# Delta stage of a four-layer kernel: a new order by hand for the products of q and the gate, the output products, the sums z, the norms and the alpha spread

## The chip, the cores and the metric

The kernel runs on one core of a Trainium2 chip. The metric is device time in microseconds (us) of one launch, the median of several. Engines: PE is TensorE (matmul), DVE VectorE, ACT ScalarE, POOL GpSimd, SP the engine whose queue issues most transfers.

## The reference

Four layers, each followed by a residual sum and a layer norm. The first is a gated delta rule over x (8 batches, 1024 steps, width 512):

```
q, kr, v = x @ Wq + bq, x @ Wk + bk, x @ Wv + bv          # 128 wide
k = kr / max(norm(kr), 1e-12)
alpha, beta, gate = sigmoid(x @ Wa + ba), sigmoid(x @ Wb + bb), sigmoid(x @ Wg + bg)
S_new = a * (S - b * outer(S k, k)) + b * outer(v, k)     # one step
o = (q @ S_new) * gate
x1 = layernorm(x + o @ Wo + bo)
```

Then three blocks of 4-bit weights with a low-rank term; an attention whose values are zero by its shapes (HD equals ROPE, so it adds nothing to x); and a low-rank MLP.

## The kernel before, in words

The first part of the program, the **delta stage** (`delta_rule_and_weights`), computes x1 and turns the packed weights into float tiles; a second part runs the two MLPs, and its code isn't changed.

The delta stage takes the 1024 steps in 8 chunks of 128 (`CHUNKS`) and the 8 batches in 2 groups of 4 (`GB`, `GROUPS`). One chunk of one group is a **unit**, numbered n = 2c + g, 0 to 15. Every engine runs the same list of pieces, `ORDER`, once per unit, taking the pieces that it has code for, in that order and without overtaking; semaphores tie the engines. In `ORDER` a word `U.0'` with one mark belongs to the unit before (n - 1), with two marks to the one before that (n - 2); so each pass works on three units. `ORDER` is used for units 0 to 13 (2 to 13 in a hardware loop of two units a turn), `ORDER_PREVIOUS` for unit 14 and `ORDER_LAST` for unit 15, both with pieces of the weights' preparation added; `TAIL` follows.

The pieces that matter here:
- xT: 4 transposes of x on PE for a batch s (L883), waiting for the load of `x_in[g]`; ACT and DVE take the high and low halves. kv: 12 products (L895 to L899) into bank `p_pj[s % 2]`; sq and copy: ACT empties it.
- root, diag, kh: 1 / norm of k and khat. DVE makes the floor (L721), POOL the power (L511) and beta's diagonal (L527), DVE khat (L742). **decay** is the alpha spread: PE spreads alpha (L939) into `p_wide` (h = 0) or `p_pj[1]` (h = 1), and DVE scans it into DT (L729) and A (L734).
- kT, kk, MnT, M, W0: the triangular system of the chunk. M (L976) transposes it, W0 ends in M_both on DVE; part.2 to part.6 are five masks of it on POOL (L533), then kA (L541) and qA (L548) follow on POOL.
- The **levels** 1 to 6 invert it by doubling. In each, PE does Y (L1003) and T (L990), ACT copies both out, PE does X (L1011), DVE adds it in (L786), and the next level's Y waits for that. `inverse` is the last half level.
- KS', U', PT', S', O': the chunk's result og for the unit before, and its new state S on DVE. ogT': og split in high and low halves by ACT and POOL (L552).
- q and g: 12 products each of 512 columns (L905), into `p_pj[0]` and `p_pj[1]`; qout and gout: ACT empties them.
- attn.s': 3 products with Wo (L1090 to L1092) for a batch s, into `p_pj[s % 2]`. z.s': DVE adds the residual (L830). stats.s: DVE's mean and variance, POOL's rstd. norm.s: DVE's `(z - mean) * rstd` in place (L843).
- residual pieces: POOL adds bo to `x_res` (L567), one with each of KS', U', PT' and S'.

The SP queue, in order, in a turn of the loop:

```
load(c + 1, 0); load(c + 1, 1)              # x_in
store(c, 0); load_residual(c + 1, 0)        # a store waits for each norm
store(c, 1); load_residual(c + 1, 1)
```

so the loads of `x_in` for units 2c + 4 and 2c + 5 stand behind the last norm of unit 2c + 1, which is done in unit 2c + 3. After the loop, ahead of the loads for unit 14 stands `load_rows(0)`, and the end of unit 15's queue is: `store(6, 1)` (the norms of unit 13), its residual, lora_b (`lb`), a wait for unit 15's g products, `load_rows(3)`, three loads of lora_a (`la`). ACT's pieces `la_hi` wait for these.

Of the kernel before, what the change touches and what calls it, by code (L numbers as in the profile page):

```python
# [117 lines left out]
def delta_rule_and_weights(nc, x, w, consts, masks, x1, q, kept):  # L118
# [22 lines left out]
    with nc.cleanup_on_exit(), ExitStack() as ctx:  # L141
# [146 lines left out]
        def order(text):  # L288
# [24 lines left out]
        def with_more(more):  # L313
# [11 lines left out]
        G_PIECES = [("g", i, 0) for i in range(3 * KT)] + [("gout", 0, 0)]  # L325
        ORDER_LAST = [piece for piece in with_more({
# [16 lines left out]
        def tail(text):
# [11 lines left out]
            stats.2' lbT.0 stats.3' lbT.1 U tile.0.0 norm.2' norm.3' lbT.2 PT low.0.0 tile.0.1 S low.0.1 tile.0.2 O low.0.2 tile.0.3 lbT.3 low.0.3  # L355
# [26 lines left out]
        def ring_free(eng, *piece):  # L382
# [114 lines left out]
        def _(pool):  # L497
# [89 lines left out]
        def _(act):  # L587
# [112 lines left out]
        def _(dve):  # L700
# [112 lines left out]
            def O(c, g, _):  # L813
# [4 lines left out]
                for s in range(GB if state_used(c) else 0):  # L818
                    dve.wait_ge(s_["S_ps"], 2 * n + s // 2 + 1)
# [44 lines left out]
            run(dve, {"xT": xT, "root": root, "decay": decay, "kh": kh, "A": A_, "MnT": MnT_, "W0": X0, "Y": Y, "X": X, "inverse": inverse, "KS": KS, "U": U, "PT": PT_, "O": O,  # L864
# [3 lines left out]
        def _(pe):  # L868
# [1166 lines left out]
```

## Time and profile before

| | us |
|---|---|
| median of 3 runs (range) | 2453.42 (2453.25 to 2454.66) |
| the profiled execution | 2452.19 |
| its span | 2450.40 |
| delta stage: to the end of unit 15 | 695.8 |
| tail of the weights' preparation | 695.8 to 738.3 |
| second part | 739.8 to 2450.4 |
| PE busy in the span | 2321.4 (95%) |
| DVE, ACT, POOL busy | 1590.2, 1146.5, 766.8 |

The span runs from the first to the last instruction of the profiled execution; its own time has 1.79 us around that. Busy time of PE is modelled to the end of each matmul, so neighbours overlap and a short gap shows only where PE really waited. "Idle before <- X" names what released an engine. A unit is counted from one unit's first transpose of x to the next one's.

### The profile page before, as it was taken

The page shows a single profiled execution, that of the slowest core. Times are in us where ns is not written, and L with a number is a line of the kernel's source. Part 1 is how long each engine was busy: PE and PEld are TensorE (multiplying, and loading weights), DVE is VectorE, ACT ScalarE, POOL GpSimd, SP SyncE. Part 2 cuts the span into 40 slices and gives each one's busy share as a digit, 9 for nine tenths or more (in the row PEclk, how much of TensorE's full clock was granted, in tenths as well). Part 3 has the DMA queues.
Part 4 walks back from the last instruction along what each step waited for, and adds up shares of the span by engine and source line. Part 5 has one row for each costly group of instructions (what it writes and reads, how often), then busy time and mean ns, then how long its engine had stood idle before and what let it go on. Part 6 is the DMA issues. An engine that isn't in the chain of part 4 may idle for free.

```text
span 2450.4 us, 37424 instructions
## 1 busy us (share of the span) xinstructions
PE 2321.4 (95%) x12333; PEld 1931.0 (79%) x12333; DVE 1590.2 (65%) x3002; ACT 1146.5 (47%) x2289; POOL 766.8 (31%) x1200
## 2 busy tenths in 40 slices
PE   6898888888879999999999999999999999999997
PEld 5787777877767888888888888888888878888886
DVE  3656565656676666666666766667676666666666
ACT  3333333333244433435344353443534477777775
POOL 2344444444441121111211112111120135555555
PEclk8999999999989999999999999999999999999999
DMA  5122122122340020100201002010021233333222
GB/s 133 52 70 82 55 93 78 43 94 94 102 153 1 18 87 1 69 34 17 86 0 68 34 17 86 0 68 34 17 94 39 86 100 112 115 114 107 103 86 69
DMA packets 101706, 166.14 MB, mean 68 GB/s; under 512 B 19664, under 2 KB 22480, under 8 KB 101520
## 3 DMA queue, kind: packets, MB, share of 16 engines
q1 hardware_dynamic: 97328, 163.69, 19.8%
q10 hardware_dynamic: 4320, 1.71, 0.3%
q8 instruction: 32, 0.52, 0.1%
q14 instruction: 26, 0.21, 0.0%
HBM read 115.05 MB, written 50.33 MB: 67 GB/s over the span
## 4 chain that ended last, share of the span: by engine, by line
PE 67%; DVE 1%; POOL 1%; issue 0%; DVEq 0%; ACT 0%; POOLq 0%
PE quant_bank L1512 7%; PE quant_bank L1511 7%; PE quant_bank L1510 7%; PE quant_bank L1900 6%; PE quant_bank L1902 6%; PE quant_bank L1901 6%; PE quant_bank L1538 5%; PE quant_bank L1537 5%; PE quant_bank L1539 5%; PE quant_bank L1527 3%; PE quant_bank L1556 2%; PE quant_bank L1558 2%; PE quant_bank L1557 2%; PE quant_bank L1499 1%; PE quant_bank L1917 1%; PE quant_bank L1568 1%
## 5 line engine op out<-in xcount | busy, mean ns | idle before, releaser
L1351 POOL TENSOR_SCALAR quant_var<-quant_mv 128x1 f32<-128x1 f32 x256 | 57.0, 223 | 1007.1 <-DVE quant_mv L1426 1007.1
L1379 ACT ACTIVATE quant_g_hi<-quant_bank,kept_beta,kept_gamma 128x512 fp32r<-128x512 f32 x192 | 150.7, 785 | 395.5 <-PE quant_bank L1527 395.4
L1510 PE MATMUL quant_bank<-kept_W_hi,quant_h_hi 128*128 128x512 f32 x768 | 305.4, 398 | 0.0
L1511 PE MATMUL quant_bank<-kept_W_lo,quant_h_hi 128*128 128x512 f32 x768 | 303.5, 395 | 0.0
L1512 PE MATMUL quant_bank<-kept_W_hi,quant_h_lo 128*128 128x512 f32 x768 | 303.4, 395 | 0.0
L1424 DVE BATCH_NORM_STATS2 quant_stats<-quant_bank 128x6 f32<-128x512 f32 x192 | 134.0, 698 | 196.3 <-PE quant_bank L1512 196.3
L1865 DVE TENSOR_TENSOR mlp_g_lo<-quant_bank,mlp_g_hi 128x512 fp32r<-128x512 f32 x256 | 176.4, 689 | 105.7 <-ACT quant_bank L1802 105.3
L1801 ACT ACTIVATE mlp_g_hi<-quant_bank,mlp_b 128x512 fp32r<-128x512 f32 x256 | 177.3, 693 | 70.6 <-PE quant_bank L1902 63.5
L1537 PE MATMUL quant_bank<-quant_g_hi,kept_W_hi 128*128 128x512 f32 x512 | 205.2, 401 | 0.0
L1538 PE MATMUL quant_bank<-quant_g_hi,kept_W_lo 128*128 128x512 f32 x512 | 202.5, 396 | 0.0
L1539 PE MATMUL quant_bank<-quant_g_lo,kept_W_hi 128*128 128x512 f32 x512 | 202.4, 395 | 0.0
L1446 DVE TENSOR_TENSOR quant_g_lo<-quant_bank,quant_g_hi 128x512 fp32r<-128x512 f32 x192 | 130.3, 689 | 100.1 <-ACT quant_bank L1380 97.9
L1394 ACT ACTIVATE quant_bank<-kept_b_all 128x512 f32<-128x512 f32 x192 | 113.2, 603 | 133.1 <-DVE quant_y L1439 74.3
L1512 PEld LDWEIGHTS quant_bank<-kept_W_hi,quant_h_lo 128*128 128x128 f32 x768 | 144.0, 187 | 35.1
L1511 PEld LDWEIGHTS quant_bank<-kept_W_lo,quant_h_hi 128*128 128x128 f32 x768 | 144.1, 188 | 34.1
L1510 PEld LDWEIGHTS quant_bank<-kept_W_hi,quant_h_hi 128*128 128x128 f32 x768 | 144.0, 188 | 34.1
L1802 ACT ACTIVATE quant_bank<-quant_bank,mlp_b 128x512 f32<-128x512 f32 x256 | 168.2, 657 | 0.0
L1439 DVE TENSOR_SCALAR quant_y<-quant_bank,quant_mv,quant_rstd 128x512 f32<-128x512 f32 x192 | 155.6, 810 | 17.3 <-POOL quant_rstd L1353 17.3
L1353 POOL TENSOR_TENSOR quant_rstd<-quant_var,quant_minus_half 128x1 f32<-128x1 f32 x256 | 141.3, 552 | 21.3
L1380 ACT ACTIVATE quant_bank<-quant_bank,kept_beta,kept_gamma 128x512 f32<-128x512 f32 x192 | 145.4, 757 | 0.0
L1389 ACT ACTIVATE quant_h_hi<-kept_x_in 128x512 fp32r<-128x512 f32 x128 | 81.9, 640 | 123.6 <-DVE kept_x_in L1458 99.7
L1760 POOL TENSOR_SCALAR mlp_z<-mlp_z,mlp_mv,mlp_rstd 128x512 f32<-128x512 f32 x60 | 124.0, 2079 | 0.0
(277 smaller groups left out, 5889.6 us busy)
## 6 DMA issues: line engine op xcount, KB each, us to landing
delta_x_in<-L_attn_x_d SPq DMA_DIRECT2D x16, 1024.0 KB, 8.0
delta_x_res<-L_attn_x_d SPq DMA_DIRECT2D x16, 1024.0 KB, 5.4
x_d<-delta_z SPq DMA_DIRECT2D x64, 256.0 KB, 2.1
kept_x_in<-x_d SPq DMA_DIRECT2D x16, 1024.0 KB, 5.3
quant_y<-x_d SPq DMA_DIRECT2D x16, 1024.0 KB, 5.2
x_d<-quant_y SPq DMA_DIRECT2D x16, 1024.0 KB, 4.2
mlp_x_in<-x_d SPq DMA_DIRECT2D x16, 1024.0 KB, 10.4
mlp_x_res<-x_d SPq DMA_DIRECT2D x16, 1024.0 KB, 6.5
```

What stands on the lines that cost most here:

```text
L1379: nc.scalar.activation(g_hi[m][:, k, :], tr[k][:, :], ACT.Gelu, bias=beta[:, b, k:k + 1], scale=gamma[:, b, k:k + 1])
L1439: nc.vector.tensor_scalar(y[m][:, e, :], lin_of["up", m, b, e][:, :], mv[m][:, e, 0:1], rstd[m][:, e:e + 1], ALU.subtract, ALU.mult).then_ ...
L1510: mm(out, x_hi, W_hi[2 * b][:, k, :], start=False, stop=False, skip_group_check=True)
L1511: mm(out, x_hi, W_lo[2 * b][:, k, :], start=False, stop=False, skip_group_check=True)
L1512: last = mm(out, x_lo, W_hi[2 * b][:, k, :], start=False, stop=k == KT - 1, skip_group_check=True)
L1537: mm(out, W_hi[2 * b + 1][:, k, cols], g_hi[m][:, k, :], start=k == 0, stop=False)
L1538: mm(out, W_lo[2 * b + 1][:, k, cols], g_hi[m][:, k, :], start=False, stop=False)
L1539: last = mm(out, W_hi[2 * b + 1][:, k, cols], g_lo[m][:, k, :], start=False, stop=k == KT - 1)
L1801: nc.scalar.activation(g_hi[:, at, :], p_h[at][:, :], ACT.Gelu_apprx_tanh, bias=b1[:, f:f + 1])
L1802: nc.scalar.activation(p_h[at][:, :], p_h[at][:, :], ACT.Gelu_apprx_tanh, bias=b1[:, f:f + 1]).then_inc(s_["gelu_done"], 1)
L1865: nc.vector.tensor_tensor(g_lo[:, at, :], p_h[at][:, :], as_f32(g_hi[:, at, :]), ALU.subtract).then_inc(s_["g_lo_done"], 1)
L1900: mm(out, lhs[0], rhs[0], start=first, stop=False)
```

## The change

- `ORDER` is written anew. The 12 products of q (now single pieces) stand in threes between kk, decay.1, kT.1, M.0 and kk.1; the 12 of g follow, all ahead of level 1. The output products attn', now three pieces each, stand two to a level in levels 1 to 5 and two in level 6; z' stands in levels 2, 4, 5 and behind `inverse`, stats.0' and stats.1' in levels 3 and 5.
- decay.0 stands behind S' and kv.2, where it stood ahead of S'. norm.0'' and norm.1'' stand behind xT.3, norm.2'' and norm.3'' in level 1, behind X.1.1. The four updates of S become pieces new_S.0 and new_S.1, with root.1 between them.
- The waits for the banks `p_pj` follow the new order: attn.0 and attn.1 wait for q and the gate of the next unit to be out, the seeds of kv for z.2 and z.3 of two units before.
- `ORDER_LAST` no longer moves g into level 1. la_hi.0 stands behind X.2.0 (it stood behind X.4.1), la_hi.1 behind X.3.0.
- The SP queue's code and the engine of the norm (DVE, L843) are not changed.

```diff
         ORDER = order("""
-            xT.0 xT.1 KS.0' kv.0 stats.0'' stats.1'' stats.2'' sq.0 copy.0 U.0' xT.2 kv.1 norm.0'' stats.3'' norm.1'' sq.1 copy.1 ab.0 PT.0' xT.3 root.0 diag.0 decay.0 kh.0
-            norm.2'' norm.3'' S.0' O.0' kv.2 sq.2 copy.2 kT.0 ogT.0' A.0 kv.3 sq.3 copy.3 root.1 ab.1 diag.1 kk.0 attn.0' MnT.0 z.0' decay.1 attn.2' kh.1 kT.1 M.0 z.2' W0.0 kk.1 q.0 q.1 A.1 MnT.1 q.2 q.3 M.1 qout.0 W0.1 attn.1'
-            part.2 part.3 part.4 part.5 part.6 kA.0 z.1' attn.3' qA.0
-            Y.1.0 T.1.0 Y.1.1 T.1.1 z.3' X.1.0 X.1.1
-            Y.2.0 T.2.0 Y.2.1 T.2.1 g.0 X.2.0 X.2.1 g.1
-            Y.3.0 T.3.0 Y.3.1 T.3.1 g.2 X.3.0 X.3.1 g.3
-            Y.4.0 T.4.0 Y.4.1 T.4.1 g.4 X.4.0 X.4.1 g.5
-            Y.5.0 T.5.0 Y.5.1 T.5.1 g.6 X.5.0 X.5.1 g.7
-            Y.6.0 T.6.0 Y.6.1 T.6.1 g.8 g.9 inverse.0 inverse.1 g.10 g.11 gout.0""")
+            xT.0 xT.1 KS.0' kv.0 sq.0 copy.0 stats.2'' U.0' xT.2 kv.1 sq.1 copy.1 ab.0 root.0 diag.0 stats.3'' PT.0' xT.3 norm.0'' norm.1''
+            S.0' kv.2 sq.2 copy.2 decay.0 kh.0 A.0 O.0' kT.0 kv.3 sq.3 copy.3 new_S.0' root.1 ab.1 diag.1 new_S.1' ogT.0'
+            q.0 q.1 q.2 kk.0 MnT.0 decay.1 q.3 q.4 q.5 kh.1 kT.1 A.1 M.0 q.6 q.7 q.8 W0.0 kk.1 q.9 q.10 q.11 qout.0 MnT.1 g.0 g.1 g.2 M.1 g.3 g.4 g.5 W0.1
+            part.2 part.3 part.4 part.5 part.6 kA.0 g.6 g.7 g.8 g.9 g.10 g.11 qA.0 
+            Y.1.0 T.1.0 Y.1.1 T.1.1 gout.0 attn.0.0' X.1.0 X.1.1 norm.2'' norm.3'' attn.0.1'
+            Y.2.0 T.2.0 Y.2.1 T.2.1 attn.0.2' X.2.0 X.2.1 z.0' attn.1.0'
+            Y.3.0 T.3.0 Y.3.1 T.3.1 attn.1.1' X.3.0 X.3.1 stats.0' attn.1.2'
+            Y.4.0 T.4.0 Y.4.1 T.4.1 attn.2.0' X.4.0 X.4.1 z.1' attn.2.1'
+            Y.5.0 T.5.0 Y.5.1 T.5.1 attn.2.2' X.5.0 X.5.1 z.2' stats.1' attn.3.0'
+            Y.6.0 T.6.0 Y.6.1 T.6.1 attn.3.1' attn.3.2' inverse.0 inverse.1 z.3'""")
...
-        G_PIECES = [("g", i, 0) for i in range(3 * KT)] + [("gout", 0, 0)]
-        ORDER_LAST = [piece for piece in with_more({
+        ORDER_LAST = with_more({
             ("norm", 1, 2): dequants((1, 0)),
             ("norm", 3, 2): dequants((1, 1)),
             ("kh", 0, 0): dequants((1, 2), (1, 3)),
             ("X", (1, 1), 0): dequants((2, 0)),
-            ("X", (2, 0), 0): [("stats", 0, 1)],
+            ("X", (2, 0), 0): [("la_hi", 0, 0)],
             ("X", (2, 1), 0): dequants((2, 1)),
-            ("X", (3, 0), 0): [("norm", 0, 1)],
-            ("X", (3, 1), 0): [("stats", 1, 1), ("lb_hi", 0, 0), ("lb_hi", 1, 0)],
+            ("X", (3, 0), 0): [("la_hi", 1, 0)],
+            ("stats", 0, 1): [("la_lo", 0, 0), ("lb_hi", 0, 0), ("lb_hi", 1, 0)],
             ("X", (4, 0), 0): dequants((2, 2)) + [("lb_hi", 2, 0), ("lb_lo", 0, 0)],
-            ("X", (4, 1), 0): [("norm", 1, 1), ("la_hi", 0, 0), ("la_lo", 0, 0)],
-            ("X", (5, 0), 0): dequants((2, 3)) + [("la_hi", 1, 0), ("la_lo", 1, 0)],
-            ("X", (5, 1), 0): dequants((3, 0)) + [("la_hi", 2, 0), ("la_lo", 2, 0)],
-            ("inverse", 0, 0): [("la_hi", 3, 0), ("la_lo", 3, 0), ("KS", 0, 0)]}) if piece not in G_PIECES]
-        at = ORDER_LAST.index(("X", (1, 1), 0)) + 1
-        ORDER_LAST[at:at] = G_PIECES
+            ("z", 1, 1): [("norm", 0, 1), ("la_lo", 1, 0), ("la_hi", 2, 0)],
+            ("X", (5, 0), 0): dequants((2, 3)) + [("la_hi", 3, 0)],
+            ("stats", 1, 1): dequants((3, 0)) + [("la_lo", 2, 0)],
+            ("inverse", 0, 0): [("la_lo", 3, 0), ("norm", 1, 1), ("KS", 0, 0)]})
...
-            stats.2' lbT.0 stats.3' lbT.1 U tile.0.0 norm.2' norm.3' lbT.2 PT low.0.0 tile.0.1 S low.0.1 tile.0.2 O low.0.2 tile.0.3 lbT.3 low.0.3
+            stats.2' lbT.0 stats.3' lbT.1 U tile.0.0 norm.2' norm.3' lbT.2 PT low.0.0 tile.0.1 S new_S.0 new_S.1 low.0.1 tile.0.2 O low.0.2 tile.0.3 lbT.3 low.0.3
...
                 elif bank is p_pj[0]:
-                    eng.wait_ge(s_["q_done"], GROUPS * CHUNKS)
+                    eng.wait_ge(z_done[2], GROUPS * CHUNKS - 1)
                 elif bank is p_pj[1]:
-                    eng.wait_ge(s_["g_done"], GROUPS * CHUNKS)
+                    eng.wait_ge(z_done[3], GROUPS * CHUNKS - 1)
...
             def la_lo(c, g, l):
                 pool.wait_ge(w_["la_hi_done"], l + 1)
-                pool.wait_ge(w_["lb_lo_done"], 1)
-                pool.wait_ge(s_["rstd_done"], GB * (GROUPS * CHUNKS - 2) + min(l + 1, 2) if l < EARLY else GB * GROUPS * CHUNKS)
+                if l >= 1:
+                    pool.wait_ge(w_["lb_lo_done"], 1)
+                pool.wait_ge(s_["rstd_done"], GB * (GROUPS * CHUNKS - 2) + 1 + l // 2 if l < EARLY else GB * GROUPS * CHUNKS)
...
                 if s < 2:
-                    wait(act, s_[("q_done", "g_done")[s]], n)
+                    wait(act, z_done[2 + s], n - 1)
...
                 dve.wait_ge(s_["O_ps"], n + 1)
                 nc.vector.tensor_tensor(og[:, :, :], small, gate[g][:, :, :], ALU.mult).then_inc(s_["og_done"], 1)
 
-                for s in range(GB if state_used(c) else 0):
-                    dve.wait_ge(s_["S_ps"], 2 * n + s // 2 + 1)
+            def new_S(c, g, h):
+
+                if not state_used(c):
+                    return
+                n = GROUPS * c + g
+                dve.wait_ge(s_["S_ps"], 2 * n + h + 1)
+                for s in (2 * h, 2 * h + 1):
                     nc.vector.scalar_tensor_tensor(S[g][:, s, :, :], S[g][:, s, :, :], A[g][:, s, P - 1:P], pair[s // 2][:, s % 2, :, :],
                                                    ALU.mult, ALU.add).then_inc(s_["S_done"], 1)
...
-            def q_(c, g, k):
-
-                n = GROUPS * c + g
-                if k == 0:
+            def q_(c, g, i):
+
+                n = GROUPS * c + g
+                if i == 0:
                     pe.wait_ge(s_["xT_lo_done"], GB * n + GB)
                     pe.wait_ge(s_["kv_done"], GB * n + 3)
-                    wait(pe, z_done[2], n)
-                for part in range(3):
-                    last = columns_product(p_q, Q_OF, k, part)
-                if k == KT - 1:
+                last = columns_product(p_q, Q_OF, i // 3, i % 3)
+                if i == 3 * KT - 1:
                     last.then_inc(s_["q_ps"], 1)
 
             def g_(c, g, i):
@@ -922,7 +924,6 @@
                 if i == 0:
                     pe.wait_ge(s_["xT_lo_done"], GB * n + GB)
                     pe.wait_ge(s_["A_done"], GB * n + GB)
-                    wait(pe, z_done[3], n)
                 last = columns_product(p_g, G_OF, i // 3, i % 3)
                 if i == 3 * KT - 1:
...
-            def attn(c, g, s):
-
-                n = GROUPS * c + g
-                pe.wait_ge(s_["ogT_lo_done"], n + 1)
-                if s >= 2:
-                    pe.wait_ge(z_done[s - 2], n + 1)
-                elif not isinstance(n, int) or n < GROUPS * CHUNKS - 1:
-                    if s == 0:
-                        pe.wait_ge(s_["kv_done"], GB * (n + 1) + 3)
+            def attn(c, g, at):
+
+                s, part = at if isinstance(at, tuple) else (at, None)
+                n = GROUPS * c + g
+                if not part:
+                    pe.wait_ge(s_["ogT_lo_done"], n + 1)
+                    if s >= 2:
+                        pe.wait_ge(z_done[s - 2], n + 1)
+                    elif not isinstance(n, int) or n < GROUPS * CHUNKS - 1:
+                        pe.wait_ge(s_[("q_done", "g_done")[s]], n + 2)
                     else:
-                        pe.wait_ge(s_["A_done"], GB * (n + 1) + GB)
-                else:
-                    ring_read(pe, p_pj[s % 2], EARLY_PIECES)
+                        ring_read(pe, p_pj[s % 2], EARLY_PIECES)
                 out = p_pj[s % 2][:, :]
-                mm(out, ogT_hi[:, s, :], wo_hi[:, :], start=True, stop=False)
-                mm(out, ogT_hi[:, s, :], wo_lo[:, :], start=False, stop=False)
-                mm(out, ogT_lo[:, s, :], wo_hi[:, :], start=False, stop=True).then_inc(attn_ps[s], 1)
+                for i, (weights, moving) in enumerate(((ogT_hi, wo_hi), (ogT_hi, wo_lo), (ogT_lo, wo_hi))):
+                    if part is None or i == part:
+                        last = mm(out, weights[:, s, :], moving[:, :], start=i == 0, stop=i == 2)
+                        if i == 2:
+                            last.then_inc(attn_ps[s], 1)
```

## Rows read from the trace of the kernel before

**Rows 1.** Windows: us, busy PE, PEld, DVE, ACT, POOL (instructions), granted clock, DMA share, GB/s.

```profile
54.70:94.80 40.10, 36.78 (x261) 32.60 (x260) 19.96 (x50) 14.81 (x50) 12.89 (x16) 1.00 0.08 28
94.80:600.10 505.30, 446.62 (x3122) 392.39 (x3121) 306.83 (x744) 177.74 (x600) 223.94 (x312) 1.00 0.22 77
600.10:643.30 43.20, 36.79 (x261) 32.56 (x260) 27.41 (x67) 14.82 (x50) 19.07 (x26) 1.00 0.23 74
643.30:695.80 52.50, 41.93 (x250) 35.47 (x249) 34.56 (x74) 18.91 (x58) 28.69 (x33) 0.90 0.41 113
739.80:2450.40 1710.60, 1695.25 (x8064) 1384.98 (x8064) 1148.91 (x1966) 882.57 (x1446) 450.55 (x767) 1.00 0.17 60
```

**Rows 2.** Waits, 94.8 to 600 us: who waited for whom, total us, times, longest.

```profile
PE delta_p_wide L939 <- DVE delta_PT L811: 21.1, 12, 1.8
PE delta_p_pj L1090 <- DVE delta_z L830: 20.1, 24, 0.9
PE delta_p_pj L1090 <- POOL delta_ogT_lo L552: 9.7, 12, 0.9
```

**Rows 3.** Timeline of PE in unit 9: start us, us, what, [idle before <- releaser].

```profile
393.64 1.13 PE L1037 MATMUL delta_p_pair<-delta_XZ,delta_bR 128*128 128x128 f32 x8 [0.16 <-DVE delta_bR L800]
...
407.08 0.65 PE L899 MATMUL delta_p_pj<-delta_w_hi,delta_xT_lo 128*128 128x258 f32 x4
...
411.71 0.44 PE L952 MATMUL delta_p_tr<-kept_ident,delta_khat 128*128 128x128 f32 x2
...
415.94 0.27 PE L976 MATMUL delta_p_tr<-kept_ident,delta_MnT 128*128 128x128 f32 x1
...
418.74 0.40 PE L1003 MATMUL delta_p_wide<-delta_XZ,delta_M_both 128*128 128x128 f32 x2
...
422.99 0.47 PE L1003 MATMUL delta_p_wide<-delta_XZ,delta_L 128*128 128x128 f32 x2
...
425.05 0.47 PE L1003 MATMUL delta_p_wide<-delta_XZ,delta_L 128*128 128x128 f32 x2
...
431.96 1.03 PE L883 MATMUL delta_p_tr<-kept_ident,delta_x_in 128*128 128x128 f32 x8
```

**Rows 4.** Timeline of DVE in unit 9.

```profile
397.38 1.16 DVE L843 TENSOR_SCALAR delta_z<-delta_z,delta_mv,delta_rstd 128x512 f32<-128x512 f32 x1
...
404.63 0.99 DVE L843 TENSOR_SCALAR delta_z<-delta_z,delta_mv,delta_rstd 128x512 f32<-128x512 f32 x2
...
411.26 0.40 DVE L742 TENSOR_TENSOR delta_khat<-delta_kvab,delta_rn 128x256 f32<-128x256 f32 x1
...
424.62 0.69 DVE L786 TENSOR_TENSOR delta_XZ<-delta_p_pair,delta_XZ 128x128 f32<-128x128 f32 x2 [1.37 <-PE delta_p_pair L1011]
```

**Rows 5.** Timelines of POOL (unit 9), then DVE, POOL and ACT (unit 15).

```profile
420.37 1.27 POOL L541 TENSOR_TENSOR delta_qkA<-delta_qkT,delta_A 128x512 f32<-128x512 f32 x1
...
675.57 1.30 DVE L856 SCALAR_TENSOR_TENSOR delta_rows<-delta_rows,delta_scale 128x512 f32<-128x512 int32 x1
...
676.27 1.75 POOL L548 TENSOR_TENSOR delta_qkA<-delta_qkT,delta_A 128x512 f32<-128x512 f32 x1
...
687.92 0.63 ACT L685 ACTIVATE delta_la_early<-delta_la_st_early 96x512 fp32r<-96x512 f32 x1 [2.82 <-DMA delta_la_st_early<-L_ffn_lora_a_d]
```

**Rows 6.** Timeline of SP's queue, in unit 9 and in unit 15.

```profile
407.30 1.03 SPq L437 DMA_DIRECT2D delta_x_in<-L_attn_x_d  x2
...
659.57 0.45 SPq L440 DMA_DIRECT2D delta_x_res<-L_attn_x_d  x1
...
678.42 0.37 SPq L450 DMA_DIRECT2D delta_rows<-L_ffn_qweights_d  x1
```

**Rows 7.** Tile views, landings: x_in issued 407.30; x_in issued 575.49; lb issued 660.46.

```profile
DMA to landing us min/median/max: 6.9/6.9/6.9
...
DMA to landing us min/median/max: 9.8/9.8/9.8
...
DMA to landing us min/median/max: 6.6/6.6/6.6
```

More of the change, by code:

```diff
@@ L862, in low @@
                 nc.vector.tensor_tensor(kept.W_lo[l][:, j, :], ring_bank("tile", i)[:, :], as_f32(kept.W_hi[l][:, j, :]), ALU.subtract).then_inc(w_["W_lo_done"], 1)
-            run(dve, {"xT": xT, "root": root, "decay": decay, "kh": kh, "A": A_, "MnT": MnT_, "W0": X0, "Y": Y, "X": X, "inverse": inverse, "KS": KS, "U": U, "PT": PT_, "O": O,
+            run(dve, {"xT": xT, "root": root, "decay": decay, "kh": kh, "A": A_, "MnT": MnT_, "W0": X0, "Y": Y, "X": X, "inverse": inverse, "KS": KS, "U": U, "PT": PT_, "O": O, "new_S": new_S,
                       "z": z_, "stats": stats_, "norm": norm, "unit": unit_, "dequant": dequant, "low": low})
```

## The prediction, made before the changed kernel was run

> **What bounds the kernel now.** I read the windows first. PE is busy in 1695 of 1711 us of the second part, which the change doesn't touch; the delta stage is where PE idles [rows 1]. Units 2 to 13 take 505.3 us, 42.1 each, of which PE is busy 446.6, 37.2 each: 4.9 us a unit are gaps. The waits over the same 12 units say what ends them [rows 2]: decay.0 waits for PT_done of the unit before (21.1 us), attn.2 and attn.3 for z.0 and z.1, whose banks they write over (20.1), attn.0 for POOL's half of og (9.7). These make 50.9 us, 4.2 a unit. The other 0.7 is small: 0.2 where U' waits for KS' [rows 3], the rest at kk.1 and at level 2. Last comes the timeline of one unit in the middle of the loop (unit 9): where on PE's order each wait lies, and in the levels how little room there is. A level takes 2.06 us from Y to Y [rows 3]; PE has work throughout, and X, DVE's addition and the next Y follow each other closely, so a late DVE lengthens a level at once. DVE has 1.37 us free between the additions of two levels [rows 4].
>
> **The 4.2 us.** All three waits go. decay.0 comes 3.3 us of PE's work (S' and kv.2) later, and its 1.8 us wait is shorter than that. attn' starts in level 1, over 6 us after og was split, and two levels lie between a z and the product that waits for it. The wait at kk.1 goes too, as six products now lie between kT.1, M.0 and it. No matmul is added or taken away, so PE's 37.2 stays.
>
> **The filler in the levels.** Before, a level held two products of g; now two of the output products, with the same 512 columns, so the level stays 2.06. On DVE, z takes 0.7 us and a statistics piece about 0.9, under the 1.37 free. Only level 5 has both, and behind it comes the longer gap ahead of `inverse`. ACT's gout (0.7) is in level 1, where ACT waits over 1 us. I cost these at nothing.
>
> **kT.1 becomes a wait.** Behind kv.3 runs a chain: ACT's square, DVE's floor, POOL's power and diagonal, DVE's decay.1 and kh.1, PE's kT.1. Before, it took from the last part of kv.3 at 407.08 (ended by about 407.6) to 411.71, 4.1 us, of which 0.35 was a z that DVE did ahead of decay.1 [rows 3]. PE spent them on kk.0, attn.0, decay.1 and attn.2. Now there are only q.0 to q.5, kk.0 and decay.1: 6 x 0.23 and the short ones, 2.3 us. In the chain the floor no longer meets a POOL operation (saves 0.3 to 0.4), but ogT on POOL now runs beside kh.1, which was 0.40 alone [rows 4] and will be some 0.4 more. Chain 3.7, less 2.3: a new wait of 1.4 us (1.0 to 1.8).
>
> **The norms in level 1 collide with POOL.** This is the step that I weigh most. A norm alone takes 0.5 us (two took 0.99), but the one at 397.38, with a residual addition running on POOL, took 1.16 [rows 4]. In unit 15 a DVE operation at 675.57, behind kA, took 1.30, and qA, issued meanwhile, took 1.75 where kA takes 1.27 [rows 5]. So these two engines shut each other out for whole operations. Where do they meet now? M.1 was at 415.94 and kA at 420.37, 4.4 later, with POOL running without a break from the masks on [rows 3, 5]. In the new order nine g products lie between M.1 and Y.1.0, so Y.1.0 (call it Y) is 2.4 behind M.1 and kA runs from Y + 2.0 to Y + 3.3, then qA. X.1.1 reaches DVE at about Y + 2.1, norm.2'' issues at Y + 2.3: it waits for kA and ends at Y + 3.6. qA has been issued, takes 1.2 more, and norm.3'' ends at Y + 5.0. Only then can DVE add X.2.0, due at Y + 3.7. Level 2 is 1.25 us longer. The low end is 0.3: norm.3'' slips in ahead of qA, or norm.2'' ahead of kA (0.25 us decides that); two such DVE operations in a row against waiting POOL work are not in the trace. I take 1.25, as qA in unit 15 started as soon as its one blocker ended.
>
> The Trainium skill ("SBUF — State Buffer", section "Who interferes with whom") says that the pair of ports these engines share is an exclusive lock, that whoever issues first has it for the whole instruction, and that the other fully blocks. By that rule qA, issued ahead of norm.3'', goes first, and the unit would be 1.25 longer; without a lock it would be 0. This trace agrees on one blocked operation (1.16 against 0.5).
>
> **A unit of the loop**: 37.2 + 0.2 (U') + 1.4 (kT.1) + 1.25 (level 2) = 40.05, against 42.1: 2.05 less, times 12 = **-24.6**.
>
> **Loads of x_in.** The norms are later in the unit, and the loads stand behind them on SP. Before, the last norm ended at 405.6 and x_in was issued at 407.30 and landed 6.9 later [rows 4, 6, 7]: 8.6 after the norm. Now that is Y + 5.0 + 8.6 = Y + 13.6. The next unit starts at Y + 13.2 (418.74 to 431.96 [rows 3]) less 0.55 for the two g that stood behind `inverse`, less 0.1, plus 1.25: Y + 13.8. It just fits; for five such starts I allow **+0.5** in all. The residual's load lands earlier still, and POOL needs it no sooner.
>
> **Units 0 and 1** have no norms of earlier units. Unit 1: 40.1 before [rows 1], PE's 36.8 + 1.6 now, -1.7. Unit 0 waits at the same places, but has no output products to fill the levels when its g leave them; I guess it by unit 1 at -1.5. Together **-3.2** (-1 to -5).
>
> **Unit 14** took 43.2, of which 1.1 was dequantisation on DVE, and that stays; one more in level 1 costs 0.5. Its x_in has 1 MB of packed weights in front and landed 9.8 instead of 6.9 after its issue [rows 7]: with no slack left, 2.9. So 40.05 + 1.1 + 0.5 + 2.9 = 44.5, **+1.3**.
>
> **Unit 15** took 52.5. ACT's la_hi.0 was in level 4 and waited 2.82 us for lora_a, to 687.92 [rows 5]. Now it is in level 2, and ACT's copies for level 3 are behind it. On SP, lora_a stands behind the norms of unit 13, now in level 1, a residual, lora_b and 1 MB of weights. With Y at 27.5 from the unit's start (26.2 by the other units, 1.3 for dequantisation) and one dequantisation more ahead of the norms, the last norm ends at Y + 5.8 and the residual is issued at Y + 6.25 = 33.8. From there to lora_b's landing is 0.9 + 6.6 = 7.5 us (659.57, 660.46 and the landing [rows 6, 7]), and from the weights' issue at 678.42 to lora_a's landing was 9.5. One behind the other these make 17.0; if their queueing hides more, 13.5. I take 15.5: lora_a lands at 49.3. From there to the end of unit 15 was 7.9 us; two levels more make 4.2, ACT's and POOL's preparation pieces, now bunched, 0.5. Its end was DVE's, 0.6 behind PE's new boundary: 49.3 + 12.6 - 0.6 = 61.3. **+8.8** (+5 to +13). The tail has the same pieces and transfers: 0.
>
> **The sum.** -24.6 + 0.5 - 3.2 + 1.3 + 8.8 = -17.2. On the profiled execution's 2452.2 that is 2435.0. The median of the runs is 1.2 above it, so I say **2436.0**.
>
> **Rivals.**
> - *The norms hardly collide* (0.3 instead of 1.25): 0.95 x 12 = 11.4 less, 2425. For: a quarter of a us decides; with the kT.1 wait at its low end 2420. Against: POOL is busy without a break there. Chance 0.27.
> - *The ends are dearer*: lora_a at 17.0 and PE at half clock behind the long stall (the clock was 0.90 of full over unit 15, with a stall of 2.8 there [rows 1, 5]), the kT.1 wait 1.8: +1.5 +2 +4.8, 2444. Chance 0.17.
> - *Slower*: x_in lands late at every second unit. Its price is the time that it is late, six times. It decides from (17.2 + 4.9) / 6 = 3.7 us: then the kernel is slower. For: the slack is 0.2. Against: landings of 6.9 repeat, and nothing else moves data then. Chance 0.04.
> - *Nothing*: the two together come near zero, from x_in late by 2.1 us up, or DVE work in levels 2 to 5 adding 0.3 to each. Chance 0.06.
>
> The forecast itself has 0.46. Its own range is 2430 to 2441. The range that leaves out 2 in 10 reaches into the first two rivals: **2421 to 2448**. About 0.2% (4.9 us) is what a measurement can tell from no change; faster 0.90, same 0.06, slower 0.04.
>
> **What would show it.** In the changed profile: no wait of decay.0, attn.0, attn.2 and attn.3 in the loop; a wait of about 1.4 us ahead of kT.1 that DVE's khat ends; norms at L847 or so of 1.2 us or more in level 1, and a gap of 1.2 us on PE at Y.3.0; units of 40.0; a first transpose in unit 14 that waits for x_in; ACT in unit 15 waiting over 12 us for lora_a, and PE behind it. I am wrong if the norms meet POOL otherwise than counted, if a unit's start waits for x_in throughout, or if lora_a comes much sooner or later than 49 us into unit 15.

## The result, and the profile after

The changed kernel takes **2415.23 us** (median of 4 runs, 2414.15 to 2416.22). The kernel before, run beside it, takes 2454.04 (4 runs, 2453.25 to 2457.15): a ratio of 0.9839 (95% interval 0.9822 to 0.9856), 38.8 us less. I had said 2436.0, range 2421 to 2448: the direction was right, and the time lies below the range. The profiled execution took 2414.36 with a span of 2412.6, so 37.8 of the span's 2450.4 are gone.

Windows of the kernel after: unit 1, units 2 to 13 with the wait ahead of unit 14, unit 14, unit 15, the second part; and below them unit 9 by itself. They answer to [rows 1].

```profile
50.90:87.50 36.60, 35.12 (x262) 32.52 (x262) 20.68 (x54) 14.92 (x50) 13.27 (x18) 1.00 0.10 30
87.50:552.50 465.00, 427.63 (x3123) 390.35 (x3122) 328.55 (x747) 179.12 (x600) 230.09 (x316) 1.00 0.23 82
552.50:595.10 42.60, 37.33 (x260) 33.69 (x261) 30.00 (x65) 14.92 (x50) 16.60 (x23) 0.96 0.25 90
595.10:657.40 62.30, 38.89 (x254) 34.46 (x253) 35.88 (x72) 19.73 (x59) 26.95 (x32) 0.84 0.31 92
701.70:2412.60 1710.90, 1694.93 (x8064) 1384.45 (x8064) 1149.56 (x1966) 882.52 (x1446) 448.49 (x767) 1.00 0.18 60
...
357.11:395.48 38.37, 35.58 (x262) 32.52 (x262) 27.29 (x63) 14.93 (x50) 18.97 (x27) 1.00 0.26 94
```

What ended PE's waits in units 2 to 13 (us in total, times, longest), for [rows 2]:

```profile
PE delta_p_tr L953 <- DVE delta_khat L741: 17.1, 12, 1.4
PE delta_p_wide L1004 <- DVE delta_XZ L785: 14.6, 12, 1.2
PE delta_p_tr L887 <- DMA delta_x_in<-L_attn_x_d: 1.3, 2, 0.8
```

| | forecast | measured | from |
|---|---|---|---|
| a unit of the loop | 40.05 | 38.4 | starts of the units |
| of it: gap at U' | 0.2 | 0.14 | unit 9 |
| gap ahead of kT.1 | 1.4 | 1.44 | unit 9 |
| gap ahead of Y.3.0 | 1.25 | 1.22 | unit 9 |
| **PE's work without gaps** | **37.2** | **35.6** | unit 9; 427.63 / 12 |
| x_in late in the loop, 12 units | +0.5 | +1.3 | waits |
| units 0 and 1 | -3.2 | -7.5 | 79.2 against 86.7 |
| x_in of unit 14 late | +2.9 | +2.7 | timeline |
| unit 14 itself | -1.6 | -0.7 | 42.6 against 43.3 |
| unit 15 | +8.8 | +9.8 | 62.3 against 52.5 |
| tail | 0 | +0.3 | 44.3 against 44.0 |

Units 2 to 13 without the 4.0 us for x_in are 44.3 shorter (505.3 - 461.0), where I had 24.6. That is 19.7 us, about the whole miss. The gaps don't explain it, since each one came out to a few hundredths. Of the 19.7, 1.3 is no gain of the change: in the profiled execution of the kernel before, unit 4 took 43.25 us at a mean granted clock of 0.96, where its neighbours took 41.96 at 1.00. The other 18.4 are 12 times 1.53, PE's work in a unit.

PE's timeline of unit 9, around the two waits (start, busy time, engine, line, out<-in, count, idle time before it). They answer to [rows 3]:

```profile
374.19 0.39 PE L909 MATMUL delta_p_pj<-delta_xT_hi,delta_w_lo 128*128 128x512 f32 x1
374.42 0.39 PE L909 MATMUL delta_p_pj<-delta_xT_lo,delta_w_hi 128*128 128x512 f32 x1
376.24 0.44 PE L953 MATMUL delta_p_tr<-kept_ident,delta_khat 128*128 128x128 f32 x2 [1.44 <-DVE delta_khat L741]
...
385.33 0.48 PE L1092 MATMUL delta_p_pj<-delta_wo_hi,delta_ogT_hi 128*128 128x512 f32 x1
387.02 0.48 PE L1004 MATMUL delta_p_wide<-delta_XZ,delta_L 128*128 128x128 f32 x2 [1.22 <-DVE delta_XZ L785]
```

DVE and POOL in the same unit: khat for kT.1, and the norms in level 1 with kA and qA ([rows 4, 5]).

```profile
375.38 0.81 DVE L741 TENSOR_TENSOR delta_khat<-delta_kvab,delta_rn 128x256 f32<-128x256 f32 x1
...
383.76 2.94 DVE L847 TENSOR_SCALAR delta_z<-delta_z,delta_mv,delta_rstd 128x512 f32<-128x512 f32 x2
386.62 0.47 DVE L785 TENSOR_TENSOR delta_XZ<-delta_p_pair,delta_XZ 128x128 f32<-128x128 f32 x2
...
374.64 1.27 POOL L550 TENSOR_TENSOR delta_ogT_lo<-delta_og,delta_ogT_hi 128x512 fp32r<-128x512 f32 x1
...
383.73 1.28 POOL L539 TENSOR_TENSOR delta_qkA<-delta_qkT,delta_A 128x512 f32<-128x512 f32 x1
384.96 1.45 POOL L546 TENSOR_TENSOR delta_qkA<-delta_qkT,delta_A 128x512 f32<-128x512 f32 x1
```

norm.2'' and norm.3'' took 2.94 us together, where two of them took 0.99 alone [rows 4]. kA (383.73 to 385.0) held up the first and qA (384.96 to 386.4) the second; DVE's addition X.2.0 came at 386.62 and Y.3.0 at 387.02. This is the order that I had counted out. The rule of the Trainium skill ("SBUF — State Buffer", section "Who interferes with whom"), that the engine which issues first has the ports for its whole instruction, agrees: qA was issued 0.25 us ahead of the second norm and went first.

Unit 15 on ACT and PE, and SP's queue ahead of it ([rows 5, 6]):

```profile
642.00 0.63 ACT L684 ACTIVATE delta_la_early<-delta_la_st_early 96x512 fp32r<-96x512 f32 x1 [17.91 <-DMA delta_la_st_early<-L_ffn_lora_a_d]
...
643.01 1.22 PE L1012 MATMUL delta_p_pair<-delta_level_L,delta_Z_both 128*128 128x128 f32 x4 [14.22 <-ACT delta_Z_both L665]
...
644.46 0.63 PE L1004 MATMUL delta_p_wide<-delta_XZ,delta_L 128*128 128x128 f32 x2
...
647.45 0.49 PE L1004 MATMUL delta_p_wide<-delta_XZ,delta_L 128*128 128x128 f32 x2
...
627.86 0.39 SPq L467 DMA_DIRECT2D delta_lb<-L_ffn_lora_b_d  x1
628.30 4.61 SPq L448 DMA_DIRECT2D delta_rows<-L_ffn_qweights_d  x1
632.95 1.84 SPq L452 DMA_DIRECT2D delta_la_st_early<-L_ffn_lora_a_d  x3
```

ACT's la_hi.0 waits 17.91 us for lora_a with the copies of level 3 behind it, and PE is without work for 14.22 us. lora_a is there 46.9 us into the unit (forecast 49.3). From there to the unit's end it is 15.4 (forecast 12.0): the first 3.6 us behind the stall run at half clock (1.2 of 2.4 GHz; the granted clock was 0.50 from 643.0 to 646.6), as the pair of Y shows that takes 0.63 at 644.46 and 0.49 again at 647.45.

### The profile page after: what moved, and what is told of

Same layout as the page of the kernel before. It is cut to its first block, busy times and chain, and to the rows that moved or that the text cites. A ratio compares the mean times of both kernels' runs of the same rounds, so it can differ in the third digit from the quotient of the medians.

```text
span 2412.6 us, 37430 instructions
## 1 busy us (share of the span) xinstructions
PE 2296.9 (95%) x12333; PEld 1926.4 (80%) x12333; DVE 1617.6 (67%) x3002; ACT 1148.3 (48%) x2289; POOL 767.2 (32%) x1200
## 4 chain that ended last, share of the span: by engine, by line
PE 68%; DVE 1%; POOL 1%; issue 0%; DVEq 0%; ACT 0%; POOLq 0%
PE quant_bank L1514 7%; PE quant_bank L1513 7%; PE quant_bank L1512 7%; PE quant_bank L1902 6%; PE quant_bank L1904 6%; PE quant_bank L1903 6%; PE quant_bank L1539 5%; PE quant_bank L1540 5%; PE quant_bank L1541 5%; PE quant_bank L1529 4%; PE quant_bank L1558 2%; PE quant_bank L1560 2%; PE quant_bank L1559 2%; PE quant_bank L1501 1%; PE quant_bank L1919 1%; PE quant_bank L1570 1%
```

## The experiments

I had two theories of the missing 19.7 us before the first experiment. **W**: a wait on PE costs more than its gap, because the profile books part of it as busy time, so seven waits made into three take busy time away as well. **P**: a wait costs its gap, and the busy time fell because of where the products stand. They are told apart by a unit's time less its gaps, which is PE's busy time in a window over unit 9 (called PE's work below, with all gaps counted, the short one at U' too). The diffs show the changed stretches of the lines of `ORDER`, not the whole lines. PE's work is 35.58 after, as shown above, and before

```profile
390.01:431.97 41.96, 37.11 (x262) 32.61 (x261) 25.53 (x63) 14.81 (x50) 18.65 (x26) 1.00 0.27 100
```

**The kernel before, with decay.0 and kh.0 behind kv.2.**

```diff
-  xT.3 root.0 diag.0 decay.0 kh.0
-  norm.2'' norm.3'' S.0' O.0' kv.2 sq.2 copy.2 kT.0
+  xT.3 root.0 diag.0
+  norm.2'' norm.3'' S.0' kv.2 sq.2 copy.2 decay.0 kh.0 O.0' kT.0
```

> The kernel before, with only decay.0 (and DVE's kh.0) moved behind S' and kv.2. Both theories expect the 1.76 us gap ahead of decay.0 to go and no other to grow by over 0.3. Theory W (a wait on PE costs its gap in the profile and some 0.25 us more, because the last matmul ahead of it is booked to its modelled end and the first behind it is slow): the loop's unit falls from 41.96 to 39.95. Theory P (a wait costs its gap; the busy time of PE fell by 1.6 us a unit in the changed kernel because of where the products stand): 40.2.

Measured: 2436.04 us in one run, beside a median of 2454.61 for the kernel before. Unit 9, and PE's waits of units 2 to 13:

```profile
383.21:424.04 40.83, 37.16 (x262) 32.68 (x261) 25.14 (x63) 14.93 (x50) 18.91 (x26) 1.00 0.28 103
...
PE delta_p_tr L952 <- DVE delta_khat L742: 10.9, 12, 0.9
PE delta_p_pj L1090 <- POOL delta_ogT_lo L552: 6.0, 12, 0.6
```

The edit moves one piece more than the expectation names: O.0' stands behind kv.2 and decay.0 too. Neither number came: the decay wait (1.75 a unit) went, but kh.0 is now later too, and a wait of 0.91 ahead of kT.0 took its place. Seven waits before, seven now, and PE's work stays at 37.16. A miss for both forecasts, since neither had counted the new wait; it fits W, but does not test it.

**The changed kernel, with kA.0 and qA.0 on POOL moved from ahead of level 1 to behind stats.0'.**

```diff
-  part.6 kA.0 g.6 g.7 g.8 g.9 g.10 g.11 qA.0
+  part.6 g.6 g.7 g.8 g.9 g.10 g.11
-  X.3.0 X.3.1 stats.0' attn.1.2'
+  X.3.0 X.3.1 stats.0' kA.0 qA.0 attn.1.2'
```

> The changed kernel, with kA.0 and qA.0 moved on POOL from behind the masks to behind stats.0' (level 3). If norm.2'' and norm.3'' are late because POOL's operations shut them out, they take 0.5 us each, the 1.22 us gap ahead of Y.3.0 goes, and a unit falls from 38.37 to 36.9 (W) or 37.15 (P), the median to about 2396. The rival, that level 1 has simply too much work for DVE, expects the gap to stay near 1.2 and the time to be the same.

Measured: 2395.1 us (2393.43 to 2397.02), ratio 0.9759 (0.9742 to 0.9775). Unit 9, and its pair of norms in level 1:

```profile
347.81:384.79 36.98, 35.42 (x263) 32.52 (x262) 25.54 (x63) 14.93 (x50) 18.81 (x27) 1.00 0.28 101
...
374.46 0.99 DVE L847 TENSOR_SCALAR delta_z<-delta_z,delta_mv,delta_rstd 128x512 f32<-128x512 f32 x2
```

The pair takes 0.99 us instead of 2.94, and the gap ahead of Y.3.0 is gone: the collision is shown, since the norms did not move. The unit falls by 1.39, the gap was 1.22: the wait cost 0.16 to 0.17 more than its gap.

**The changed kernel, with the norms moved instead.**

```diff
-  kv.0 sq.0 copy.0 stats.2'' U.0' xT.2 ... PT.0' xT.3 norm.0'' norm.1''
+  kv.0 sq.0 copy.0 stats.2'' norm.0'' norm.1'' U.0' xT.2 ... PT.0' xT.3 norm.2'' norm.3''
-  X.1.0 X.1.1 norm.2'' norm.3'' attn.0.1'
+  X.1.0 X.1.1 attn.0.1'
```

> The changed kernel, with norm.0'' and norm.1'' behind stats.2'' and norm.2'' and norm.3'' behind xT.3, none in level 1. The gap ahead of Y.3.0 goes (unit 36.9 by W, 37.15 by P). SP's queue runs some 12 us earlier: the 2.74 us wait for x_in at unit 14 goes, and the wait for lora_a in unit 15 falls from 14.2 to about 4. Together 32 us less: 2383. If the transfers had nothing to do with the ends, only the 12 to 14 units' gaps would go: 2396.

Measured: 2378.31 us (2377.49 to 2380.14), ratio 0.9691 (0.9675 to 0.9708). Unit 9:

```profile
347.23:384.22 36.99, 35.43 (x262) 32.51 (x262) 25.53 (x63) 14.91 (x50) 19.20 (x27) 1.00 0.31 113
```

The loop gains what it gained from moving kA. The other 20 us are mostly at the ends: SP's loads stand behind the last norm, so unit 14's x_in is no longer waited for (from unit 13's start to 14's 37.0 instead of 41.3), unit 14 is 4.3 shorter, and from unit 15's start to the second part it is 94.6 instead of 106.6; PE's gap for lora_a is 4.8 instead of 14.2. The kernel with kA later, which has no collision either but leaves the norms in level 1, kept all of this: 2.3 us of waiting for unit 14's x_in, a gap of 14.3 in unit 15, 106.5 us to the second part. So it is the place of the norms that sets when the queue moves on, and with it the stall for lora_a.

**The changed kernel, with DVE's kh.1 ahead of decay.1.**

```diff
-  MnT.0 decay.1 q.3 q.4 q.5 kh.1 kT.1
+  MnT.0 kh.1 decay.1 q.3 q.4 q.5 kT.1
```

> The changed kernel, with DVE's kh.1 ahead of decay.1. If kT.1 waits for the chain by way of decay.1, the 1.44 us gap ahead of it falls to about 0.35, a unit to 37.3, the median to 2400. If it is the power on POOL alone that khat waits for, the gap stays over 1.2 and the time is the same.

Measured: 2397.57 us (2394.32 to 2399.25), ratio 0.9766 (0.975 to 0.9782).

```profile
347.61:384.78 37.17, 35.61 (x263) 32.53 (x262) 26.79 (x63) 14.92 (x50) 19.17 (x27) 1.00 0.27 96
...
PE delta_p_tr L953 <- DVE delta_khat L741: 2.6, 13, 0.2
```

The wait became short (0.2) but did not go, and PE's work stayed at 35.61: the unit fell by 1.20, as the gap did by 1.24. What lies above the gap is a price of each wait, the same for one of 1.44 and one of 0.20.

**The changed kernel, with decay.0 and kh.0 back ahead of S': one wait more.**

```diff
-  PT.0' xT.3 norm.0'' norm.1''
-  S.0' kv.2 sq.2 copy.2 decay.0 kh.0 A.0
+  PT.0' xT.3 norm.0'' norm.1'' decay.0 kh.0
+  S.0' kv.2 sq.2 copy.2 A.0
```

> The changed kernel with decay.0 and kh.0 back ahead of S' (behind norm.1''), and nothing else: a wait for PT_done of the unit before comes back on PE, and the products stay where they are. Theory W (each wait on PE costs its gap and 0.15 to 0.25 us more, which the profile books as busy time): a unit less its gaps goes from 35.6 to 35.75 or 35.85. Theory P (the busy time fell because of where the output products and those of q and the gate now stand): it stays at 35.6, and the unit grows by the gap alone.

Measured: 2430.77 us in one run. Unit 9, and PE's waits of units 2 to 13:

```profile
367.37:406.82 39.45, 35.82 (x263) 32.50 (x262) 27.60 (x63) 14.92 (x50) 18.96 (x27) 1.00 0.25 90
...
PE delta_p_wide L940 <- DVE delta_PT L810: 10.4, 12, 0.9
```

No product but decay.0's own two moved, and PE's work rose by 0.24. This is W's number; P's, no change, did not come.

**The kernel before, with only the pieces around its waits moved.**

```diff
-  kv.3 sq.3 copy.3 root.1 ab.1 diag.1 kk.0 attn.0' MnT.0 z.0' decay.1 attn.2' kh.1 kT.1 M.0 z.2' W0.0 kk.1
-  q.0 q.1 A.1 MnT.1 q.2 q.3 M.1 qout.0 W0.1 attn.1' part.2 ... kA.0 z.1' attn.3' qA.0
+  kv.3 sq.3 copy.3 kT.0 ogT.0' A.0 root.1 ab.1 diag.1 kk.0 MnT.0 decay.1 kh.1 attn.0' z.0' kT.1 M.0 W0.0 kk.1
+  attn.2' z.2' A.1 attn.1' MnT.1 z.1' q.0 M.1 q.1 q.2 q.3 qout.0 W0.1 attn.3' part.2 ... kA.0 qA.0
```

(decay.0, kh.0 and O.0' stand behind kv.2, as in the first experiment.)

> The kernel before, with q and the gate where they stood (q behind kk.1, the gate in the levels), and only the pieces around the waits moved: decay.0 behind kv.2, attn.0' behind kh.1, attn.2' and attn.1' behind kk.1, attn.3' behind the last of q. The waits of decay.0, attn.2, attn.3 and kk.1 go (3.7 us) and one of about 2 us ahead of kT.1 comes: 7 gaps in a unit become 3 or 4. Theory W: a unit less its gaps falls from 37.1 to 36.3 to 36.6, although no product has moved into or out of the levels. Theory P: it stays at 37.1.

Measured: 2488.4 us in one run, slower than the kernel before. Units 8 and 9, and PE's waits of units 2 to 13:

```profile
364.80:411.10 46.30, 41.01 (x262) 35.49 (x261) 25.77 (x63) 14.70 (x50) 18.93 (x26) 0.89 0.13 45
411.08:453.57 42.49, 37.12 (x262) 32.66 (x260) 25.75 (x63) 14.70 (x50) 18.93 (x26) 1.00 0.27 99
...
PE delta_p_pj L1090 <- DVE delta_A L734: 18.5, 12, 1.6
PE delta_p_tr L952 <- DVE delta_khat L742: 17.7, 12, 1.5
PE delta_p_pj L1090 <- POOL delta_ogT_lo L552: 10.3, 12, 0.9
PE delta_p_small L962 <- ACT delta_qkT L655: 9.5, 12, 0.8
```

As a test of W it failed: three waits went (decay.0, attn.2, attn.3) and three came (kk.0, kT.1, and attn.1 for DVE's scan of A), so there are seven again and 5.4 us of gaps. It says one thing: with seven waits and the output products elsewhere, PE's work is 37.12, against 37.11 before. Moving them about ahead of the levels gives nothing; inside the levels they were not tried here.

**The changed kernel, with q.0 to q.2 directly behind kv.2: a wait ahead of a wide product.**

```diff
-  S.0' kv.2 sq.2 copy.2 decay.0 ...
-  q.0 q.1 q.2 kk.0 MnT.0
+  S.0' kv.2 sq.2 copy.2 q.0 q.1 q.2 decay.0 ...
+  kk.0 MnT.0
```

> The changed kernel with q.0, q.1 and q.2 moved up, directly behind kv.2, where they wait for ACT to empty the bank; nothing else moves. The earlier runs put a wait ahead of a short product at its gap and 0.16 to 0.24 us. In the kernel before three of the seven waits stood ahead of products of 512 columns. If such a wait costs more than one ahead of a short product (the 512 column product no longer starts 0.08 us early behind a short one, and the one after it starts 0.08 late), a unit less its gaps goes from 35.58 to 35.9 or 36.0 with this one wait more, and three of them explain most of what is left of the 1.5 us. If a wait is a wait, it goes to 35.75 or 35.8, and the rest of the 1.5 us is from the places of the products.

Measured: 2446.82 us in one run. Unit 9, and PE's waits of units 2 to 13:

```profile
375.82:415.96 40.14, 36.03 (x263) 32.53 (x262) 27.19 (x63) 14.91 (x50) 18.94 (x27) 1.00 0.24 89
...
PE delta_p_pj L909 <- ACT delta_kvab L631: 9.9, 12, 0.8
PE delta_p_pj L940 <- ACT delta_ab L638: 6.3, 12, 0.5
```

Two waits came, not one: decay.1 now waits too (with the norms' collision, U' and kT.1 that makes five). PE's work rose from 35.58 to 36.03, 0.23 for each. If decay.1's cost the 0.16 to 0.24 of other short products, that ahead of the wide one cost 0.21 to 0.29: dearer by less than I had expected.

**The changed kernel, with lora_a's pieces behind all levels of unit 15.**

```diff
-            ("X", (2, 0), 0): [("la_hi", 0, 0)],
+            ("T", (6, 1), 0): [("la_hi", 0, 0), ("la_hi", 1, 0), ("la_hi", 2, 0), ("la_hi", 3, 0)],
-            ("X", (3, 0), 0): [("la_hi", 1, 0)],
...
-            ("stats", 1, 1): dequants((3, 0)) + [("la_lo", 2, 0)],
+            ("stats", 1, 1): dequants((3, 0)) + [("la_lo", 0, 0), ("la_lo", 1, 0), ("la_lo", 2, 0)],
```

> The changed kernel with the pieces that wait for lora_a moved behind all the levels of unit 15 (ACT's four la_hi behind T.6.1, POOL's three la_lo behind stats.1'). Theory of the stall: PE's gap of 14.2 us in unit 15 is ACT's la_hi.0, which waits 17.9 us for lora_a with the copies for level 3 behind it. Then that gap is gone; lora_a still lands 49 us into unit 15, about where the levels now end, so a wait of a few us shows ahead of the inverse or at the start of the tail, and the stretch from unit 15's first transpose to the second part goes from 106.6 to 95 to 99 us: 2404 to 2408. Rival: the tail needs lora_a soon and the stall only moves there: 2413 to 2415.

Measured: 2412.09 us (2411.35 to 2412.61), ratio 0.9823 (0.9808 to 0.9838). ACT in unit 15, and PE there and in the tail:

```profile
635.50 1.15 ACT L679 ACTIVATE delta_lb<-delta_lb 128x512 fp32r<-128x512 f32 x2 [5.39 <-DMA delta_lb<-L_ffn_lora_b_d]
...
637.03 1.22 PE L1011 MATMUL delta_p_pair<-delta_level_L,delta_Z_both 128*128 128x128 f32 x4 [5.02 <-ACT delta_Z_both L664]
...
657.60 1.88 PE L1061 MATMUL delta_p_small<-delta_PT,delta_khat 128*128 128x128 f32 x8 [4.25 <-DVE delta_PT L809]
```

The gap of 14.22 is gone, as said, but the gain is 3 us and not 7 to 11. lora_b, loaded just ahead of lora_a, is late as well: ACT waits 5.39 for it and PE 5.02, and 4.25 more come in the tail. Unit 15 to the second part: 102.6 instead of 106.6. The stall was the whole queue's lateness, of which lora_a was the last item. Both forecasts missed (2404 to 2408, and 2413 to 2415 for a stall that only moves); the second was nearer.

**All three edits together: norms at the head, kh.1 first, lora_a's pieces late.**

> The changed kernel with the norms at the head of the unit, kh.1 ahead of decay.1, and lora_a's pieces behind the levels. If the three costs are separate they add: a unit of 36.98 less 1.2 is 35.8, with the gaps ahead of Y.3.0 gone and that ahead of kT.1 at 0.2; from 2378.3 of the kernel with the norms at the head that is 14 x 1.2 = 17 less, and 0 to 4 us more from unit 15: 2358 to 2362. Rival: with both waits gone another chain (the levels on ACT and DVE, or the wait at U') sets the unit at over 36.4: 2370.

Measured: **2356.6 us** (5 runs, 2354.72 to 2357.84), ratio **0.9594** (0.9581 to 0.9607): 99 us below the kernel before and 59 below the changed one.

```profile
337.69:373.47 35.78, 35.44 (x263) 32.53 (x262) 25.04 (x63) 14.91 (x50) 19.44 (x27) 1.00 0.32 117
...
PE delta_p_tr L952 <- DVE delta_khat L740: 2.4, 12, 0.2
```

That is 2 us under the 2358 to 2362 I had expected. The unit is 35.78, which is the 36.99 with the norms at the head less kh.1's 1.20: the costs add. From unit 15's start to the second part it is 90.6, against 94.6 with the norms alone: 1.2 of it is kh.1's, which leaves 2.8 for lora_a's late pieces.

**The last one, with level 1 left without an output product between T and X.**

```diff
-            Y.1.0 T.1.0 Y.1.1 T.1.1 gout.0 attn.0.0' X.1.0 X.1.1 attn.0.1'
+            Y.1.0 T.1.0 Y.1.1 T.1.1 gout.0 X.1.0 X.1.1 attn.0.0' attn.0.1'
```

> The fastest kernel so far (norms at the head, kh.1 first, lora_a's pieces late; unit 35.76, two short gaps, 35.42 without them) with one edit: attn.0.0' stands behind X.1.1, so that level 1 has no output product between its T and X, as in the kernel before. There X.1.0's three first products took 0.3 us longer than their like in the other levels, in steps too short to show as gaps. If that is the rest of the 1.5 us that the waits do not explain, the unit grows by 0.2 to 0.3 us with no new gap. If a product's place there costs nothing, the unit stays at 35.8, and 0.3 us or more of the 1.5 us has no cause that a run shows.

Measured: 2359.14 us in one run. Unit 9:

```profile
338.37:374.28 35.91, 35.58 (x262) 32.51 (x262) 25.04 (x63) 14.96 (x50) 19.44 (x27) 1.00 0.31 117
```

0.14 to 0.15 us more, booked as work, with no new gap. So the place of a product does count a little where X follows T directly, by half of what I had expected. It is one run, but its units repeat: 4 to 13 took 35.89 to 35.93, against 35.74 to 35.77 without the edit.

## Why the prediction was wrong, step by step

**The step that failed** is one sentence: "No matmul is added or taken away, so PE's 37.2 stays." The count was right (262 in the window over unit 9 in both kernels), and the conclusion was not. What the profile calls PE's busy time is not a sum of fixed prices. The rows show it: 374.19 and 374.42 are the starts of two products of q, 0.23 apart, yet each is shown as 0.39 long, to its modelled end. In a running stream the 0.16 of overlap is counted once. Ahead of a wait no other product overlaps it, and it becomes busy time: from 374.42 to 376.24 are 1.82 us, of which a running stream needs 0.23, so the wait cost 1.59 and its gap says 1.44. Behind it the pair at kT.1 takes 0.44, where kT.0's, which waits for nothing, takes 0.38.

| kernel | waits in a unit | PE's work | unit 9 |
|---|---|---|---|
| before | 7 | 37.11 | 41.96 |
| before, decay later | 7 | 37.16 | 40.83 |
| before, waits moved | 7 | 37.12 | 42.49 |
| after, q early | 5 | 36.03 | 40.14 |
| after, decay back | 4 | 35.82 | 39.45 |
| after | 3 | 35.58 | 38.37 |
| after, kh.1 first | 3 | 35.61 | 37.17 |
| after, norms at head | 2 | 35.43 | 36.99 |
| after, kA later | 2 | 35.42 | 36.98 |
| all three | 2 | 35.44 | 35.78 |
| all three, level 1 bare | 2 | 35.58 | 35.91 |

**How much of the 1.53 it is.** Seven waits became three. Those that went on balance are the three ahead of the wide output products (0.21 to 0.29 each by q.0's) and one ahead of a short one (0.16 to 0.24): 0.8 to 1.1 us by the experiments. Level 1's missing product makes 0.15. That is 0.95 to 1.25 of the 1.53, and no experiment has the other 0.3 to 0.6. The starts in unit 9 of the kernel before have it, since two more waits there were too short to leave a gap:

```profile
390.88 1.06 PE L1028 MATMUL delta_p_wide<-delta_S,delta_qkA 128*128 128x128 f32 x8
391.81 0.36 PE L895 MATMUL delta_p_pj<-delta_w_hi,delta_xT_hi 128*128 128x258 f32 x1
...
411.38 0.39 PE L1092 MATMUL delta_p_pj<-delta_wo_hi,delta_ogT_lo 128*128 128x512 f32 x1
```

The eight products of KS' take 0.93 from the first start to that of kv.0; after the change they take 0.81. From 411.38 to kT.1 at 411.71 [rows 3] are 0.33, where a running stream needs 0.23, and the pair behind it takes 0.44 as after a wait. Together these two cost 0.27. Read in the same way, start by start, the six waits that went cost 0.21 (decay.0), 0.27, 0.24 and 0.24 (attn), 0.26 (kk.1) and 0.25 (Y.2.0) besides their gaps, and the two that came 0.21 (kT.1) and 0.17 (Y.3.0): 1.09. With level 1's 0.15 that is 1.51 of the 1.53. So W is shown by waits added and removed, and the starts of one unit give its size; the two short waits were not removed by themselves.

**The 4.2 us of waits.** Right in full: none of the three is left in the waits after.

**The filler in the levels.** Right: in unit 9's levels PE has no gap but that ahead of Y.3.0.

**kT.1 becomes a wait.** Right, 1.44 for 1.4. As I had said, khat beside ogT took 0.81 for 0.40 alone.

**The norms collide with POOL.** Right, 1.22 for 1.25, shown by moving either side. The rival "the norms hardly collide" would have come nearer to the time, for a reason that is not so.

**Loads of x_in.** Unit 14's wait was 2.7 for 2.9; in the loop 1.3 for 0.5, in two places.

**Units 0 and 1.** The failed step again: PE's work in unit 1 is 35.12 where I had kept 36.8 [rows 1], and its gaps are 1.5, where I had 1.6. Unit 0 is 4.0 shorter, guessed at 1.5 by unit 1's number.

**Unit 14.** With the lower base it would have been 40.0, and it is 42.6. Its waits are 1.3 ahead of kT.0, 2.0 ahead of kT.1 and 1.8 ahead of Y.3.0, where the loop has 0, 1.4 and 1.2: 2.5 us more, of waits for DVE, which has the dequantisation, where I had allowed 1.6. PE's work is 37.33, 1.7 over the loop's, at a granted clock of 0.96.

**Unit 15.** The stall came where I had said, with ACT waiting 17.91 where I had "over 12". lora_a was 2.4 us earlier than forecast and the rest 3.4 longer, of which the 3.6 us at half clock make about 1.8 (an estimate: half of them). I had put that into a rival only.

**The sum.** With 35.6 in place of 37.2 in units 0 to 14 my own terms give -17.2 - 15 x 1.6 = -41.2; measured -37.8. The other terms were together some 3 us too low, 2.6 of it in unit 14, and by luck this hid a little of the failed step.

## What to carry to other kernels

Price a wait of TensorE, in a stream like this one, at its gap and 0.2 us more, and count waits as well as their length: removing one is worth more than shortening one by as much. Where a change removes many short waits, don't carry the busy time over as a constant; take starts of instructions, from one to the next, instead of busy times. And when a piece is moved, ask first what stands behind it in a queue: here moving four norms forward, the last two by 17 us of a 38 us unit, was worth 37 us, 17 for a collision in twelve units and some 20 for loads far from them.

## What was not expected of the hardware

The granted clock fell without any long stall. In the kernel with the moved waits, each even unit ran at a mean clock of 0.89, with 41.01 us of PE work, and each odd one at 1.00 with 37.12, though the gaps were the same (5.3 and 5.4). Within unit 8 it was PE's thin stretch that came first:

```profile
380.00:385.00 5.00, 2.58 (x14) 1.53 (x13) 3.92 (x11) 1.53 (x6) 2.55 (x3) 1.00 0.55 193
385.00:390.00 5.00, 3.16 (x11) 2.10 (x11) 2.65 (x9) 0.38 (x1) 0.00 (x0) 0.64 0.00 0
390.00:395.00 5.00, 4.39 (x11) 3.47 (x12) 2.19 (x7) 0.00 (x0) 0.42 (x1) 0.50 0.00 0
```

PE was busy in 2.58 and 3.16 of two stretches of 5 us, and the clock went to 0.64 and 0.50 and was back at 1.00 from 400 us on (0.84 from 395 to 400). This costs 3.8 us every second unit, and explains most of why that kernel is slower than the one before. The thin stretch alone does not decide it: unit 9 has it too, with PE busy in 2.04 and 3.16 of the two stretches of 5 us from 427 on, and kept 1.00. The kernel with q.0 early also loses clock in every second unit from unit 6 on: unit 8 took 41.71 at a mean clock of 0.96, unit 9 40.14 at 1.00. Why one unit falls and the next does not stays open.
